# A post-norm transformer layer on eight Trainium2 cores: quantizing the last unit within the down projection ahead of it, twelve weight buffers after the attention, and the two norms of a unit interleaved

## What is computed

```python
x = layernorm(x + attention(x))   # 16 heads, causal, low-rank keys and values
# feed-forward part, with int8-like activations and ternary weights
def bitlinear(x, w):
    return act_quant(x) @ weight_quant(w).T
def act_quant(x):
    scale = 127 / max(max_row(abs(x)), 1e-5)
    return clip(round(x * scale), -128, 127) / scale
gate = silu(bitlinear(x, w_gate))          # 1024 -> 4096
up = bitlinear(x, w_up)                    # 1024 -> 4096
y = bitlinear(gate * up, w_down)           # 4096 -> 1024
x = layernorm(x + y)
```

## Time and profile before

| what | us |
|---|---|
| median of three runs | 1638.44 |
| the three runs | 1637.69 to 1682.19 |
| the profiled execution | 1643.48 |
| span of its slowest core, which the trace shows | 1641.9 |
| spans of the eight cores | 1625.1 to 1641.9 |
| share of the span: TensorE 79%, ScalarE 50%, VectorE 49%, GpSimd 19% | |

### The profile page before, as it was taken

One profiled execution on the slowest core, in us unless ns is written; L12 is line 12 of the kernel. 1 busy time (PEld: TensorE's weight loads), 2 busy tenths in 40 slices (PEclk: granted clock), 3 DMA queues, 4 the chain that ended last, 5 costly groups with the idle time before them and its releaser, 6 DMA issues.

```text
span 1641.9 us, 22928 instructions; the slowest of 8 cores (1625.1 to 1641.9 us)
## 1 busy us (share of the span) xinstructions
PE 1302.4 (79%) x7494; PEld 438.3 (27%) x7494; DVE 806.2 (49%) x1158; ACT 824.7 (50%) x998; POOL 317.9 (19%) x350
## 2 busy tenths in 40 slices
PE   1676675788666888979869898989868999898966
PEld 0221121122111222222212222222223444343422
DVE  2227875468447766143561434143347762635522
ACT  2577564878784676657546686768601210111100
POOL 1024412033020304121123003130220020202021
PEclk8876686567556998989979998999989999898978
DMA  9995765779595785523255232523165585765646
GB/s 249 275 274 168 224 213 192 172 250 276 188 272 191 259 231 157 130 80 101 85 159 130 90 91 73 159 81 105 60 179 197 176 209 189 169 206 155 187 138 159
DMA packets 146514, 283.07 MB, mean 172 GB/s; under 512 B 91744, under 2 KB 92000, under 8 KB 133088
## 3 DMA queue, kind: packets, MB, share of 16 engines
q1 hardware_dynamic: 144816, 272.70, 54.6%
q0 software_dynamic: 1584, 8.91, 3.5%
HBM read 235.96 MB, written 33.55 MB: 164 GB/s over the span
## 4 chain that ended last, share of the span: by engine, by line
PE 51%; DVE 18%; issue 11%; ACT 8%; DMA 7%; POOL 3%; SPq 1%; DVEq 1%; ACTq 0%; POOLq 0%
PE ps_w L986 14%; PE ps_w L1109 6%; PE ps_sc L827 6%; ACT PT L840 5%; PE ps_den L782 4%; PE ps_sc L986 4%; PE ps_pv L793 3%; PE ps_sc L1109 3%; DVE S L775 3%; DMA R<-scr_w 2%; PE ps_w L547 2%; DVE st L690 2%; DMA R<-R 2%; DVE qb L382 2%; PE ps_w L714 2%
## 5 line engine op out<-in xcount | busy, mean ns | idle before, releaser
L840 ACT ACTIVATE PT<-ps_sc,negM 128x1024 bf16<-128x1024 f32 (+3 forms) x640 | 592.7, 983 | 197.6 <-PE ps_sc L827 195.3
L986 PE MATMUL ps_w<-R,S 128*128 128x512 fp8e4 x1280 | 336.1, 393 | 34.0 <-DVE R L1005 20.3
L827 PE MATMUL ps_sc<-qn,khat 32*128 32x512 bf16 (+3 forms) x1280 | 200.4, 397 | 63.5 <-ACT PT L840 58.7
L848 POOL TENSOR_TENSOR PT<-PT,tri 128x512 bf16<-128x512 bf16 x64 | 80.3, 1254 | 530.4 <-ACT PT L840 528.7
L986 PEld LDWEIGHTS ps_w<-R,S 128*128 128x128 bf16 x1280 | 106.4, 99 | 210.2 <-issue 121.0
L782 PE MATMUL ps_den<-PT,ones 128*32 128x512 bf16 (+3 forms) x1280 | 131.7, 402 | 18.4 <-DVE S L771 10.3
L853 POOL TENSOR_SCALAR PT<-PT,hflag_sb 128x512 bf16<-128x512 bf16 x64 | 112.9, 1763 | 111.0 <-ACT PT L840 110.9
L793 PE MATMUL ps_pv<-PT,vtok 128*32 128x512 bf16 (+3 forms) x1280 | 130.6, 398 | 0.1
L1109 PE MATMUL ps_w<-R 128*128 128x512 fp8e4 x416 | 114.2, 401 | 14.1 <-DMA R<-R 11.2
L986 PE MATMUL ps_sc<-R,S 128*128 128x512 fp8e4 x512 | 116.3, 386 | 8.8 <-DMA R<-scr_w 8.7
L1005 DVE SCALAR_TENSOR_TENSOR R<-R,ps_w 128x512 f32<-128x512 f32 x80 | 54.8, 685 | 137.2 <-ACT R L999 137.2
(11 more groups left out here) (182 smaller groups left out, 1379.2 us busy)
## 6 DMA issues: line engine op xcount, KB each, us to landing
R<-scr_w SPq DMA_DIRECT2D x192, 512.0 KB, 4.5
R<-wffn SPq DMA_DIRECT2D x69, 1024.0 KB, 7.6
scr_w<-qb SPq DMA_DIRECT2D x48, 256.0 KB, 6.6
khat<-wffn SPq DMA_DIRECT2D x9, 1024.0 KB, 15.0
vtok<-wffn SPq DMA_DIRECT2D x9, 1024.0 KB, 7.8
R<-xt POOLq DMA_DIRECT2D x7, 1024.0 KB, 13.7
R<-scr_x SPq DMA_DIRECT2D x12, 512.0 KB, 5.8
y<-R SPq DMA_DIRECT2D x12, 512.0 KB, 7.4
```

What stands on the lines that cost most here:

```text
L827: t = pe(lambda e, j=j, gi=gi, tc=tc, kc=kc, stc=stc: e.matmul(ps_sc[:, j * 512 + stc:j * 512 + 512], khat[32 * j:32 * j + 32, kc:kc + 128 ...
L840: t = act(lambda e, hf=hf, pp=pp, stc=stc: e.activation(PTr[pp][:, 2 * hf:2 * hf + 2, stc:512], PSr[:, 2 * hf:2 * hf + 2, stc:512], AF.Exp ...
L848: t = pool(lambda e, pp=pp, stc=stc: e.tensor_tensor(PTr[pp][:, :, stc:stc + 128], PTr[pp][:, :, stc:stc + 128], tri.rearrange("p (r n) -> ...
L986: t = pe(lambda e, c=c, b=b, kw=kk[w], i=i: e.matmul(wring.bufs[b], xqT[u % 2][:, i * 1024 + c * 128:i * 1024 + c * 128 + 128], wbuf[kw][: ...
```

## The change

Three edits, and small ones that go with them.

1. `quant_parts` of unit 7 is called right after its up projection, and all its eight parts go into down(6), two at each `kk` of its first half. down(7) follows down(6) with nothing between and with no parts in it.
2. Once the attention is over, eight weight buffers `wb0` to `wb7` are added in the memory that it gave back. `wslot` gives the buffer of a load (first the eight new ones, then the old four, in turn), `ahead` makes `load_w` run twelve buffers ahead.
3. The two `norm2` of a unit become one block: stats and aggregate of tile 0, stats and aggregate of tile 1, and only then the application to tile 0 and to tile 1, with a statistics area of its own for each. This is for all eight units.

With it, the residual loads of `setA` and `setB` get semaphores of their own.

```diff
         def layernorm_stats(src, p):
...
+            return norm_factor(t, p)
+
+        def norm_factor(t, p):
+            t1 = dve(lambda e: e.bn_aggr(mv[:, 4 * p:4 * p + 2], st6[:, 12 * p:12 * p + 12]), [t])
...
+        more = {"first": None, "order": []}
+
+        def wslot(n):
+
+            if more["first"] is None or n < more["first"]:
+                return n % NW
+            return more["order"][(n - more["first"]) % len(more["order"])]
+
+        def ahead():
+            return len(more["order"]) or NW
+
...
-                load_w(nw[0] + NW)
+                load_w(nw[0] + ahead())
...
-            def norm2(i):
+            t_rs = [None, None]
+            for i in range(2):
+                p = 1 + i
+                for hh in range(2):
+                    t = dve(lambda e, i=i, hh=hh, p=p: e.bn_stats(
+                        st6[:, 12 * p + 6 * hh:12 * p + 6 * hh + 6],
+                        hs.x1[i][:, hh * 512:hh * 512 + 512]), [t_r2[i][hh]])
+                t_rs[i] = norm_factor(t, p)
+            for i in range(2):
...
-            norm2(0)
-            yield 0
-            norm2(1)
             yield 0
...
+            for k in range(8):
+                wb = sb(f"wb{k}", [128, 1024], F32)[:]
+                wbuf4.append(wb)
+                wbuf.append(wb.bitcast(FP8))
+                w_free.append(list(t_att_end))
+            more["first"], more["order"] = nwl[0], list(range(NW, NW + 8)) + [
+                (nwl[0] + k) % NW for k in range(NW)]
...
                 t_am = yield from up(v, hs, between)
+                parts = []
+                if v == 7:
+                    parts, out7 = quant_parts(v, hs, t_am)
                 if last is not None:
-                    yield from down(last[0], last[1], out)
+                    yield from down(last[0], last[1], out, parts)
+                    parts = []
                 last = (v, hs, t_am)
-            parts, out = quant_parts(last[0], last[1], last[2])
-            for p in parts[:2]:
-                p()
-            yield from down(last[0], last[1], out, parts[2:])
+            yield from down(last[0], last[1], out7, parts)
             put_stores()
```

More of the change, by code:

```diff
@@ L171, in build_nc @@
         xsC = sb("xsC", [128, 16], F32)
-        st6 = sb("st6", [128, 2 * 12], F32)
-        mv = sb("mv", [128, 2 * 4], F32)
+        st6 = sb("st6", [128, 3 * 12], F32)
+        mv = sb("mv", [128, 3 * 4], F32)
         sm = sb("sm", [128, 4], F32)
@@ L685, in layernorm_stats @@
         def layernorm_stats(src, p):
-            tt = []
             for hh in range(2):
-                tt.append(dve(lambda e, hh=hh: e.bn_stats(
-                    st6[:, 12 * p + 6 * hh:12 * p + 6 * hh + 6], src[hh][0]), [src[hh][1]]))
-            t1 = dve(lambda e: e.bn_aggr(mv[:, 4 * p:4 * p + 2], st6[:, 12 * p:12 * p + 12]), tt)
+                t = dve(lambda e, hh=hh: e.bn_stats(
+                    st6[:, 12 * p + 6 * hh:12 * p + 6 * hh + 6], src[hh][0]), [src[hh][1]])
+            return norm_factor(t, p)
+        def norm_factor(t, p):
+            t1 = dve(lambda e: e.bn_aggr(mv[:, 4 * p:4 * p + 2], st6[:, 12 * p:12 * p + 12]), [t])
             t2 = pool(lambda e: e.tensor_scalar(mv[:, 4 * p + 3:4 * p + 4],
@@ L881, in attention @@
                 yield 3
-        qWf = [sem(f"qWf{k}") for k in range(NW)]
+        qWf = [sem(f"qWf{k}") for k in range(NW + 8)]
         w_up = [s for io in range(8) for s in (io, 8 + io)]
@@ L892, in build_nc @@
         qXt = [sem("qXt0"), sem("qXt1")]
-        qX1 = [sem("qX1a"), sem("qX1b")]
+        qX1 = [[sem(f"qX1{a}{i}") for i in range(2)] for a in "AB"]
         qY = [sem("qYa"), sem("qYb")]
@@ L909, in load_w @@
                 n = nwl[0]
-                k = n % NW
+                k = wslot(n)
                 while wlist[n] >= 16 and st["item"] < len(order):
@@ L921, in __init__ @@
                 self.h = h
+                self.sems = sems
                 self.hqT = [e, h[0][:, 0:2048].bitcast(BF16)]
@@ L976, in up @@
                     try_prologue(u + 1)
-                kk = [nw[0] % NW, (nw[0] + 1) % NW]
+                kk = [wslot(nw[0]), wslot(nw[0] + 1)]
                 tw = [t_wl[nw[0]], t_wl[nw[0] + 1]]
@@ L1079, in x1_load @@
                 ti = 2 * u + i
-                ts.append(dma("sync", hs.x1[i], sx1[ti * 128:ti * 128 + 128, :], qX1[i],
+                ts.append(dma("sync", hs.x1[i], sx1[ti * 128:ti * 128 + 128, :], hs.sems[i],
                               hs.free[1] + [t_x1s[ti]]))
@@ L1095, in down @@
                 for kk in range(4):
-                    load_w(nw[0] + NW)
-                    kw, tw = nw[0] % NW, t_wl[nw[0]]
+                    load_w(nw[0] + ahead())
+                    kw, tw = wslot(nw[0]), t_wl[nw[0]]
                     nw[0] += 1
@@ L1131, in down, with store @@
             in_down[0] = False
-            def norm2(i):
+            t_rs = [None, None]
[7 more added lines that the diff above has]
+            for i in range(2):
                 ti = 2 * u + i
-                p = 1
-                t_rs = layernorm_stats([(hs.x1[i][:, hh * 512:hh * 512 + 512], t_r2[i][hh])
-                                        for hh in range(2)], p)
-                t = dve(lambda e: e.tensor_scalar(
+                p = 1 + i
+                t = dve(lambda e, i=i, p=p: e.tensor_scalar(
                     hs.x1[i], hs.x1[i], mv[:, 4 * p:4 * p + 1], mv[:, 4 * p + 2:4 * p + 3],
-                    ALU.subtract, ALU.mult), [t_rs])
-                def store():
+                    ALU.subtract, ALU.mult), [t_rs[i]])
+                def store(ti=ti, i=i, t=t):
                     ty = dma("sync", dy[ti * 128:ti * 128 + 128, :], hs.x1[i], qY[i], [t])
@@ L1158, in build_nc @@
         later = []
-        setA = HSet(h0, hE, None)
+        setA = HSet(h0, hE, qX1[0])
         def ffn():
@@ L1189, in ffn @@
             hB = [sb("hB0", [128, 4096], F32), sb("hB1", [128, 4096], F32)]
[L1190 removed]
+            setB = HSet([hB[0][:], hB[1][:]], sb("hBE", [128, 4096], BF16)[:], qX1[1])
             setB.free = [list(t_att_end), list(t_att_end)]
             setB.e_free = list(t_att_end)
+            for k in range(8):
[5 more added lines that the diff above has]
+                (nwl[0] + k) % NW for k in range(NW)]
             wlist[nw[0]:] = w_up + (w_up + w_down) * (7 - u) + w_down
```

1 line of the change is left out of this document (removed).

## The result

The changed kernel takes 1582.16 us (median of four runs, 1582.0 to 1583.59). Against the kernel before the ratio is 0.9648, with a 95% interval of 0.962 to 0.9676: 3.5% faster. In a second set of runs, beside the experiments, it took 1581.75 us, ratio 0.9637 (0.9624 to 0.965).

A forecast was written before the change was run, and what follows sets the result against it. TensorE's idle time and lower clock were taken to bound the part behind the attention. 25 + 3.5 + 23.4 + 2.0 + 5 = 58.9 us gave 1579.5 from the median; with 2.5 us kept back, 1582 us, range 1573 to 1604.

The forecast's parts named there:

- the 2.5 us kept back: Whole program: 2.5 us held back from the forecast for waits between the new stages that the earlier trace cannot show.
- From up(5) to down(6): Three up and three down projections: twelve buffers remove 25 of 26.2 us in and behind gaps; lower end 15 us.
- The step on the banks: Start of up(6): VectorE returns the second PSUM bank with 3.0 us of room, 2.0 more interleaved, growing from there.
- The first rival: up(5) to down(6): the load wait turns into a wait for VectorE or banks, losing 25 us: 1607 us; chance 0.08.
- The history of the gaps: Early up(6), up(7): loads stand in SyncE's queue behind transposes waiting for VectorE, giving gaps of 6.91 and 7.64 us.
- up(4): Start of up(4): 3.5 us won, between -1 and 4.4; the 2.06 us load gap stays, the 0.93 us one goes.
- The last unit: down(7): follows down(6) without its gaps and slower clock, winning 23.4 us; lower end 20.
- the cover: down(6) hides unit 7's quantization: last transpose at +29 us, needed at +38; delayed evictions do not reach the end.
- The norms at the end: End of program: interleaving takes 2.0 us off VectorE, all on the path; at least 1.0 us.
- The norms in the attention: Up projections following down projections, three places: 6 us, counted as 5 for ScalarE's pace, between 0 and 8.
- The last quantization too late: Transposes in down(6) take 9 us a pair, not 6.4: some 5 us lost, 1587 us; within the forecast's 0.88.
- The lower clock: From up(4) on: dense matmuls lower the clock to 0.79, adding 88 us: 1670 us; chance 0.04.

The follow-up runs named there:

- the kernel with the early buffers: Changed kernel with its eight buffers added and filled at once when the attention ends, in the middle of down(3), not after it; 1591.75 us, ratio 0.9695.

## Why the prediction was right

The forecast was 1582 us and the measured median is 1582.16. That the two agree so closely is partly luck. The terms below are read on core 6, as in the prediction. There they come to 63 us instead of 58.9, since the term for the attention was too small, and the span of core 6 is 64.1 us shorter. But core 6 had the longest waits. The mean core won 57.9 us by the marks, and the kernel 58 to 60 us by its ratios, from the 1641 to 1643 us that the kernel before took as a median of the later runs. The forecast counted 56.4 us from 1638.44. A term too small, a core with more to win than the others, a starting value that was 3 to 5 us low and the 2.5 us kept back cancelled.

- *From up(5) to down(6)*, predicted 25 of 26.2 us: there is no gap left, so all 26.2 went. The step on the banks held where the text looked. up(6) starts at 1377.4 us on core 2 and needs its second bank 15.5 us later, at 1392.9; L1031 gave it back at 1388.3, so 4.6 us of room, against 5.0 in the text. What the text says next, that the room grows from there, was wrong: it left out VectorE's wait for a transpose in the middle of the unit, and the room goes down to 1.7 to 3.5 us. The first rival named that wait; it came, and found just enough room. The history of the gaps was told half right: the queue stood still, but four buffers were also too few for loads of 11 us beside transposes, which the text had only as small gaps that land just late.
- *up(4)*, predicted 3.5 us: it took 64.9 us on core 6 and now takes 61.3 (1230.38 to 1291.68 us), 3.6 less. The wait for VectorE lost 1.2 us (1.41 instead of 2.65), the slow matmuls behind it are gone with 1.7, and so is the 0.93 us; the wait for the weight load stayed, as the prediction had it, and grew by 0.5 us (2.58 instead of 2.06). That the burst does not slow this load is seen from its landing, 6.7 us after its issue against 6.9.
- *The last unit*, predicted 23.4 us: down(7) follows without a gap, so 23.4. The times of the cover were also near: residual load issued at + 25.6 us (predicted + 27), first eviction at + 29.2 (+ 33), norms through at + 38.3 (+ 41). The last transpose landed at + 27.7 (+ 29). What the step didn't see is whose gain it is. The sum of the edits came out since it counted the stage once, but alone the edit gives 14 us and not 23.
- *The norms at the end*, predicted 2.0 us: 1.7 to the end of the work. The term is off by the small GpSimd instruction of tile 1, see below. To the end of the program it is 1.3 us, by the 0.4 us that the end takes longer: 8.8 us from the end of the last eviction, where the text expected about 8. The text blames such a loss on the stores coming closer together. The runs do not bear that out: the kernel with the norms in a row has 3.4 us there as well, and the interleaved ones with four or six buffers have 3.0. The cause is open.
- *The norms in the attention*, predicted 5 us: this is the term that was mis-sized. Between the profiles of before and after the attention lost 8 us, and undoing it there gives back 6.4 to 6.9 us. The two gaps of the earlier trace rows lost 2.2 and 2.5 us, and the four matmuls behind each another 0.85 us, as they no longer ran at the lower clock: 3.0 and 3.3 us a place, where the text had 2.0 and a part of the slow matmuls, 6 us for three places. The deduction for ScalarE's pace was wrong too. On core 6 up(4) starts 10.2 us sooner, where the text had about 5. The 2.5 us that I kept back for new waits were not needed for any.
- *The rivals.* The load wait that turns into another: not seen. The last quantization too late: its pairs landed 5 to 7 us apart, not 9, and the last at + 27.7, 10 us ahead of the + 38 at which the text had its need. The lower clock: over 271 us of matmuls without a gap the granted clock was 1.00, and it was 1.00 on all eight cores from 1300 to 1565 us. By that the rule of the Trainium skill (TensorE: Matmul & The Clock Gate, the section on seeing it yourself), 13/16 of the clock once three cores of a die run dense matmuls, was not met in this execution.

## What to carry to other kernels

Where loads, transposes and stores share one queue, read what stands ahead of the late load before giving it more memory; then ask how long a load takes beside the traffic of that moment, since the depth must cover the standstill and the landing together (here six buffers gave four fifths of the gain, twelve all of it). A prefetch of several MB is free only if nothing that is waited for stands behind it; the same eight buffers were worth 31 to 33 us after down(3) and 8 to 10 us less when filled at once within it. Room in a ring of banks has to be followed through the whole stage: here it was least in the middle, behind VectorE's wait for a transpose, and not at the start. And when two edits act on one stage, undo each alone: their gains are not a sum.

## What the runs showed of the hardware that I had not expected

The tiny GpSimd instruction L695 on 128x1 takes 0.22 us alone and 0.62 us when it starts while VectorE applies the norm of the other tile (the row at 1574.96 us above): 0.4 us lost of the 2.0 that the interleaving should give. This is so six times on every core of the changed kernel, and never with the norms in a row, where all 32 take 0.22 or 0.23 us.

A store of 512 KB takes 2.6 us from issue to landing with nothing beside it. A load of 512 KB takes 3.2 us at the quiet start of down(6) in the changed kernel, and 11 us in the kernel that issues its loads from ScalarE's queue, beside transposes and stores.

Eight loads, and two more behind them, in front of a transpose cost TensorE 10 us (13.25 instead of 3.4). This is what the DMA engines moved in that stretch of the kernel with the early buffers, 1185 to 1215 us in 40 slices:

```profile
GB/s 0 0 0 0 0 0 0 0 82 208 393 311 229 246 240 300 317 311 224 333 246 317 306 322 415 404 377 415 426 398 265 167 264 261 295 311 170 181 85 210
```

From 1191 to 1208 us it is some 300 GB/s, which is the 5 MB of the ten loads. By the Trainium skill (DMA: Bandwidth & Descriptors, section on queues, rings and completion order) each DMA engine consumes one queue in ring order; this agrees with the transpose that landed behind the ten loads, 13.7 us after its issue, and with the load ahead of the burst in up(4), which took 6.3 us with the burst behind it and 6.9 us in the kernel before without.
